# Half of a selective scan moved beside the relative-bias attention, and softmax division moved behind the value product

## The chip, the cores and the metric

One NeuronCore of a Trainium2 chip runs the whole program; the metric is the device time in microseconds (us) of one execution. Eight sequences go through it one after another. PE is TensorE, DVE VectorE, ACT ScalarE, POOL GpSimd, SP the engine whose queue issues all DMAs here. "BANKS" is PSUM (eight banks of 128x512 f32, PS[0] to PS[7]), WF and WB hold all constants in SBUF.

## The reference, cut to what matters

A residual stream x of shape (8, 512, 128) passes eight layers. The two that the change concerns:

```python
x = x + _L0_attn_ref(_layernorm(x), ...)        # bidirectional selective scan (Mamba)
    # per direction, 256 channels x 16 states, 512 time steps
    h = jnp.exp(dlt[:, :, None] * A) * h + (dlt * xt)[:, :, None] * bt[:, None, :]
    y = jnp.einsum('bdn,bn->bd', h, ct)
    ...
    y = (ys.transpose(1, 0, 2) + Dp * xc) * jax.nn.silu(z)
x = x + _L1_attn_ref(_layernorm(x), ...)        # 16 heads of 64, no 1/sqrt(d), relative-position bias
    attn = softmax(q @ k.T + bias[bucket(k - q)]);  out = (attn @ v) @ Wo
x = x + _L2_ffn_ref(_layernorm(x), ...)         # g1, be1, g2, be2 are layer norm gains and shifts
    x1 = _layernorm(x + attn_out, g1, be1)
    return _layernorm(x1 + moe_out, g2, be2)
```

## The kernel before

Each sequence goes through the stages moe0, attn1 (the relative-bias attention), lora1, heads (two attentions of 16 heads of 8) and last (L2's experts, L3's memory layer and experts). Six sequences run in a loop, the seventh and eighth behind it; their tiles have the prefixes y and z. While sequence b is in heads, the scan of sequence b+1 runs beside it (`mamba_scan`); its inputs were made beside the previous last stage (`mamba_pre`). The eighth has no successor: its stages run without a scan. So seven scans run beside heads, and the first runs alone (stage s0).

**The order of work.** Every engine has one queue in program order. Where two streams share a stage, each is a generator that yields nominal times, and `in_turn` merges them by these times when the program is built. The nominal times set the order and nothing else; on the chip every engine takes its queue in order and waits on semaphores.

**The scan** has 64 steps: 2 directions x 2 channel tiles x 16 states. Step m needs a decay exp(delta*A) (ACT, L754), a drive du*B (for even steps PE spreads the row of B over the partitions, L729, and DVE multiplies, L795; for odd steps a DMA brings the row and POOL multiplies, L766), the recurrence itself (DVE, L804), the product with the row of C (POOL, L770), and PE adds the product into the PSUM bank SUM by an identity matmul (L737, two passes). After 16 states DVE empties SUM (`flush`).

**attn1** handles 64 units of one head and 128 queries: PE makes a score tile (L2075), DVE adds the bias from a Toeplitz tile in `toep` and takes the row minimum (L2177), ACT exponentiates and sums the row into `den` (L2148), DVE takes the reciprocal (L2182) and multiplies the 128x512 tile `prob` by it (L2184), PE transposes it (L2082), ACT copies it to `probt` (L2156), and PE weighs the values with it (L2096, L2111). Eight units are a pair of heads; per pair PE also makes q, k and v (L2046, L2050), ACT moves them (L2127, L2130) and empties the weighed tile PS[5] to `ot` (L2137), and PE projects it (L2057) into PS[6], which adds up over all pairs; DVE adds it to X once (L2187). After step 64 of 72 only the last units' transposes, weighing and projection are left.

**last** begins with the norm ln1 (gain g1, shift be1), whose result goes through PE and ACT/DVE copies to XT, and has a norm ln2 (gain g2, shift be2) after the first experts, then XO = X + XN, a copy X <- XM (the next sequence), and ln3.

Of the kernel before, what the change touches and what calls it, by code (L numbers as in the profile page):

```python
# [18 lines left out]
ALU = mybir.AluOpType  # L19
# [19 lines left out]
H = 16  # L39
# [32 lines left out]
def bass_mk_seq(nc, x, cols_f, cols_b, ends, wf, wb, lora, lora_cols, onehot, table, w2, out):  # L72
# [35 lines left out]
    bc_dram = nc.dram_tensor("bc_rows", [2, 2 * NS, SEQ], F32, kind="Internal").ap()  # L108
    bias_dram = nc.dram_tensor("bias_line", [H, 1024], F32, kind="Internal").ap()
# [284 lines left out]
    def norm_parts(st, tag, src, dst, small, at, dst_t=None, banks=None, rms=False, sq=None, gain_t=None, gain=None,  # L394
                   shift=None, after=None, spare=None, idle=0, later=(), scaled_by_act=False):
# [12 lines left out]
        def vector(dve):  # L408
# [19 lines left out]
            if scaled_by_act:  # L428
                for j in range(NJ):
                    last = V.tensor_scalar(dst[:, j, :], src[:, j, :], s_mv[:, j, 0:1], None, ALU.subtract)  # L430
                last.then_inc(centred, 1)
            else:
                yield at + 3.2
                dve.wait_ge(rooted, 1)
            for j in range(0 if scaled_by_act else NJ):
                if rms:
# [4 lines left out]
                if gain is None:  # L441
                    ins.then_inc(normed, 1)
            if gain is not None:
                link(ins)
                link(V.tensor_tensor(dst[:, :, :], dst[:, :, :], bc(gain.unsqueeze(1), [P, NJ, D]), ALU.mult))
                V.tensor_tensor(dst[:, :, :], dst[:, :, :], bc(shift.unsqueeze(1), [P, NJ, D]), ALU.add).then_inc(normed, NJ)  # L446
            if dst_t is not None:
                yield at + 4.6
                dve.wait_ge(turned, NJ)
                if gain_t is not None:  # L450
# [19 lines left out]
        def scalar(act):  # L470
# [10 lines left out]
            if gain_t is not None:  # L481
# [9 lines left out]
    def mamba_pre(st, fetch, delay=0.0, stretch=1.0):  # L491
# [19 lines left out]
        def sync(sp):  # L511
            yield -3.0
# [164 lines left out]
    def mamba_scan(st, dest, START, STEP):  # L677

        STEPS = 2 * ND * NS
# [16 lines left out]
        def step(i):  # L696

            return i // (ND * NS), i // NS % ND, i % NS
# [22 lines left out]
        def tensor(pe):  # L721
            for s in range(STEPS + LATE):
# [8 lines left out]
                if m >= 0:  # L731
                    n = m % NS
                    yield at(s) + 0.45 * STEP
                    pe.wait_ge(rd, m + 1)
                    if n == 0 and m:
                        pe.wait_ge(emptied, m // NS)
                    nc.tensor.matmul(SUM, ident, work[:, m % RW, :], start=(n == 0), stop=(n == NS - 1)).then_inc(acc, 1)  # L737
# [8 lines left out]
        def scalar(act):  # L746
            for m in range(STEPS):
# [5 lines left out]
                a = (d * ND + t) * NS + n  # L753
# [18 lines left out]
        def vector(dve):  # L772
# [3 lines left out]
            def flush(q):  # L776
                d, t = q // ND, q % ND
                dve.wait_ge(acc, NS * (q + 1))
# [4 lines left out]
                dve.wait_ge(emptied, q)  # L783
                V.scalar_tensor_tensor(xc[:, 1, t, :], xc[:, 1, t, :], W("D")[:, ND + t:ND + t + 1], SUM,
                                       ALU.mult, ALU.add).then_inc(emptied, 1)
                dve.wait_ge(emptied, q + 1)
# [3 lines left out]
            for s in range(STEPS):  # L790
# [5 lines left out]
                if s >= NS and n == LATE:  # L796
                    yield at(s) + 0.2 * STEP
                    flush(s // NS - 1)
# [11 lines left out]
            V.tensor_tensor(dest[:, :, :], XIN[:, :, :], OUT.rearrange(tiles, j=NJ), ALU.add)  # L810

# [362 lines left out]
    def last_layers(st, copy_next):  # L1174
# [5 lines left out]
                         spare=PS[7], idle=10)  # L1180
# [8 lines left out]
        ln2 = norm_parts(st, "ln2", Y, XN, SMALL, 73.0, gain=W("g2"), shift=W("be2_2"))  # L1189
# [25 lines left out]
        def vector(dve):  # L1215
# [4 lines left out]
            nc.vector.tensor_tensor(XO[:, :, :], X[:, :, :], XN[:, :, :], ALU.add).then_inc(freed, 1)  # L1220
            if copy_next:
                dve.wait_ge(freed, 1)
                nc.vector.tensor_copy(X[:, :, :], XM[:, :, :])
            for layer in (ln3, memo, ln4, moe3):
# [348 lines left out]
    def back_parts(st, tag, heads, O, turned_o, w_o, add_to, banks, at, bias=None):  # L1573
# [21 lines left out]
        def gpsimd(pool):  # L1595
            if bias is not None:
                yield at - 24.0
                nc.gpsimd.tensor_tensor(add_to[:, :, :], add_to[:, :, :], bc(bias.unsqueeze(1), [P, NJ, D]), ALU.add).then_inc(biased, 1)

# [244 lines left out]

    with Stage("p0") as st:
# [16 lines left out]
    def layers(b, scan_next, pre_next):  # L1862
# [113 lines left out]
        with Stage("attn1") as st:  # L1976
# [5 lines left out]

            PAIR = 2 * NJ
            U, NPAIR = H * NJ, H // 2
            EXP, TURN = 2, 4
            MAKE_AT = {0: 0, 2: 1, 4: 2}
            WEIGH_AT = {5: 0, 7: 1, 1: 2, 3: 3}
            EMPTY_AT, PROJECT_AT = 4, 6  # L1990
            LAST = U + PAIR
            NS_, NP_, NT_ = 4, 6, 2 * PAIR
            RING = (PS[4], PS[7])
            qk = st.sb("qk", [P, 2, 2, SEQ])
# [417 lines left out]
```

## Time and profile before

| | us |
|---|---|
| median of 3 runs | 5484.77 |
| lowest, highest | 5479.66, 5489.24 |
| the profiled execution, its span | 5479.63, 5477.8 |

The profiled execution took 1.8 us more than the span of its instructions. A view of windows has a line for each stretch: its length, then the busy us (and number of instructions) of PE, PE's weight loads, DVE, ACT and POOL, the mean granted TensorE clock as a share of 2.4 GHz, the DMA engines' busy share, and GB/s. A view of groups has line, engine, operation, tiles and shapes, count, then total busy us and mean ns of one, then the engine's idle us ahead of them and who ended it. A timeline has start and duration in us. Engines are pipelined, so a next instruction of the same engine may start up to about 0.1 us before the one ahead ends by the record.

### The profile page before, as it was taken

To read this page: it belongs to the slowest core of one execution; us is meant where nothing else is said; L and a number is where in the kernel's file an instruction comes from. 1 tells how busy PE (TensorE), PEld (TensorE's weight loads), DVE (VectorE), ACT (ScalarE), POOL (GpSimd) and SP (SyncE) were. 2 spreads that over 40 slices of the span, in tenths; PEclk is the share of its full clock that TensorE was granted. 3 is DMA by queue.
4 is the path that set the end of the run, shared out by engine and by line. 5 is a ranking of instruction groups with operands and counts; after the bars stand their busy time and mean duration, and the time that the engine had idled before them with its cause. 6 is when DMAs were issued, how large, how long until landed. Compare 5 with 4: busy or idle time off the path is not lost. (4 is left out here: it accounts for less than half of the span.)

```text
span 5477.8 us, 69802 instructions
## 1 busy us (share of the span) xinstructions
PE 4692.1 (86%) x22038; PEld 2198.6 (40%) x22038; DVE 3509.5 (64%) x8259; ACT 2756.3 (50%) x5134; POOL 1480.0 (27%) x1876
## 2 busy tenths in 40 slices
PE   4679897998889887898878988799887998989888
PEld 2134344443444324443344433454334443444344
DVE  5766856668556784667755687556865568466445
ACT  2256553555536554375542655446654465436453
POOL 2712720136100461106401074011730127200200
PEclk8899998999989999899989999899988999999799
DMA  3411320123101231013210132001320113201000
GB/s 131 148 35 59 117 63 1 47 67 114 48 3 55 75 110 34 3 55 98 87 34 16 41 120 83 17 30 47 123 68 9 36 58 114 66 2 55 1 28 7
DMA packets 150490, 315.67 MB, mean 58 GB/s; under 512 B 16209, under 2 KB 24913, under 8 KB 150113
## 3 DMA queue, kind: packets, MB, share of 16 engines
q1 hardware_dynamic: 150128, 311.17, 17.9%
q8 instruction: 189, 3.10, 0.2%
q14 instruction: 173, 1.41, 0.1%
HBM read 307.89 MB, written 3.21 MB: 57 GB/s over the span
## 5 line engine op out<-in xcount | busy, mean ns | idle before, releaser
L196 PE MATMUL BANKS<-WB 128*128 128x512 bf16 x1616 | 448.0, 428 | 188.2 <-DVE XN L446 56.5
L770 POOL TENSOR_TENSOR heads_work<-heads_work,heads_c_all 128x512 f32<-128x512 f32 x384 | 487.1, 1271 | 325.3 <-DVE heads_work L804 312.6
L1516 ACT ACTIVATE heads_prob<-BANKS 128x512 f32<-128x512 f32 (+3 forms) x768 | 376.8, 518 | 284.6 <-PE BANKS L1411 278.2
L212 POOL TENSOR_TENSOR rstd<-rstd,WF 128x4 f32<-128x4 f32 x24 | 24.2, 1007 | 1658.2 <-DVE rstd L230 1658.2
L737 PE MATMUL BANKS<-heads_work,WF 128*128 128x512 f32 x768 | 441.0, 660 | 0.4
L196 PEld LDWEIGHTS BANKS<-WB 128*128 128x128 bf16 x1616 | 165.3, 107 | 432.1 <-issue 199.5
L406 POOL TENSOR_TENSOR rstd<-rstd,WF 128x4 f32<-128x4 f32 x48 | 48.5, 1010 | 938.5 <-DVE rstd L427 937.7
L1411 PE MATMUL BANKS<-heads_parts_kT,heads_parts_qT 64*128 64x512 bf16 (+3 forms) x768 | 237.8, 359 | 67.9 <-DVE heads_nmax L1557 47.3
L1554 DVE CUSTOM_DVE_ANT_0 BANKS<-BANKS,WF 128x384 f32<-128x384 f32 (+3 forms) x512 | 243.4, 502 | 68.9 <-PE BANKS L1411 65.6
L2156 ACT COPY attn_probt<-BANKS 128x512 f32<-128x512 f32 x384 | 223.9, 583 | 126.1 <-PE BANKS L2082 123.7
L2177 DVE CUSTOM_DVE_ANT_0 attn_biased<-BANKS,attn_toep 128x512 f32<-128x512 f32 x384 | 263.1, 685 | 34.1 <-DMA attn_toep<-bias_line 25.4
L2148 ACT ACTIVATE attn_prob<-attn_biased,attn_nmax 128x512 f32<-128x512 f32 x384 | 280.2, 730 | 1.1 <-DVE attn_nmax L2177 1.0
L882 PEld LDWEIGHTS BANKS<-last_x_w,last_x_a 128*128 128x128 f32 x1536 | 211.5, 203 | 171.7 <-ACT last_x_a L922 89.8
L882 PE MATMUL BANKS<-last_x_w,last_x_a 128*128 128x128 f32 x1536 | 219.8, 289 | 66.5 <-ACT last_x_a L922 66.5
L1557 DVE TENSOR_REDUCE heads_nmax<-BANKS 128x1 f32<-128x512 f32 x384 | 248.2, 680 | 36.9 <-PE BANKS L1411 35.2
L804 DVE TENSOR_TENSOR_SCAN heads_work<-BANKS,heads_work 128x512 f32<-128x512 f32 x192 | 233.4, 1215 | 32.6 <-POOL heads_work L766 32.6
L766 POOL TENSOR_TENSOR heads_work<-heads_b_all,m_du 128x512 f32<-128x512 f32 x192 | 244.6, 1274 | 13.7 <-DMA heads_b_all<-bc_rows 13.5
L2082 PEld LDWEIGHTS BANKS<-WF,attn_prob 128*128 128x128 f32 x1536 | 163.3, 140 | 209.2 <-DVE attn_prob L2184 134.7
L2082 PE MATMUL BANKS<-WF,attn_prob 128*128 128x128 f32 x1536 | 240.1, 281 | 6.7 <-ACT attn_probt L2156 3.7
L795 DVE TENSOR_TENSOR BANKS<-BANKS,m_du 128x512 f32<-128x512 f32 x256 | 179.6, 702 | 101.4 <-PE BANKS L729 99.7
L754 ACT ACTIVATE BANKS<-m_delta,WF 128x512 f32<-128x512 f32 x256 | 177.1, 692 | 106.6 <-DVE s_work L804 87.6
L1411 PE MATMUL BANKS<-heads_qm,heads_parts_kT 64*128 64x512 bf16 (+3 forms) x768 | 215.3, 357 | 13.4 <-DVE heads_nmax L1554 10.0
(892 smaller groups left out, 10541.3 us busy)
## 6 DMA issues: line engine op xcount, KB each, us to landing
heads_c_all<-bc_rows SPq DMA_DIRECT2D x384, 256.0 KB, 3.2
heads_b_all<-bc_rows SPq DMA_DIRECT2D x192, 256.0 KB, 3.6
attn_toep<-bias_line SPq DMA_DIRECT2D x96, 448.0 KB, 4.3
last_x_w<-in_w SPq DMA_DIRECT2D x48, 512.0 KB, 3.8
s_c_all<-bc_rows SPq DMA_DIRECT2D x64, 256.0 KB, 3.3
yheads_c_all<-bc_rows SPq DMA_DIRECT2D x64, 256.0 KB, 3.1
s_b_all<-bc_rows SPq DMA_DIRECT2D x32, 256.0 KB, 3.7
yheads_b_all<-bc_rows SPq DMA_DIRECT2D x32, 256.0 KB, 3.5
```

Source lines behind the costliest of these rows:

```text
L196: nc.tensor.matmul(bank, ident_b, bc(ident_b[:, 0:1], [P, SEQ]), start=True, stop=True)
L737: nc.tensor.matmul(SUM, ident, work[:, m % RW, :], start=(n == 0), stop=(n == NS - 1)).then_inc(acc, 1)
L766: nc.gpsimd.tensor_tensor(work[:, s % RW, :], b_all[:, k % RB, :], du[:, d, t, :], ALU.mult).then_inc(drv[1], 1)
L770: nc.gpsimd.tensor_tensor(work[:, m % RW, :], work[:, m % RW, :], c_all[:, m % RC, :], ALU.mult).then_inc(rd, 1)
L882: last = nc.tensor.matmul(DOWN[e % 2][:, j * D:(j + 1) * D], a1[:, i % 3, j * P:(j + 1) * P], down_part(i), start=(t == 0 and j == 0), sto ...
L1411: nc.tensor.matmul(take(kind, i)[:, lo:hi], left[rows, P * tile:P * (tile + 1)], right[rows, lo:hi], start=True, stop=True).then_inc(sem, 1)
L1516: nc.scalar.activation(prob[:, i % PR, lo:hi], bank("T", i)[:, lo:hi], ACT.Exp).then_inc(exped, 1)
L1554: V.tensor_tensor_reduce(got, got, W("early")[:, SEQ - hi:], -1.0, BIG, ALU.add, ALU.min, nmax[:, j, h:h + 1]).then_inc(maxed, 1)
L1557: V.tensor_reduce(nmax[:, j, h:h + 1], got, AX.X, ALU.max, negate=True).then_inc(maxed, 1)
L2082: last = nc.tensor.transpose(bank[:, kt * P:(kt + 1) * P], prob[:, u % NP_, kt * P:(kt + 1) * P], ident)
L2148: nc.scalar.activation(prob[:, e % NP_, :], biased[:, e % NS_, :], ACT.Exp, bias=nmax[:, e:e + 1], scale=-1.0, accum_out=den[:, e:e + 1]). ...
L2177: V.tensor_tensor_reduce(biased[:, s % NS_, :], PS[s % NS_], toep[:, h % 4, c:c + SEQ], -1.0, BIG, ALU.add, ALU.min, nmax[:, s:s + 1]).the ...
```

## The change

Steps 0 to 31 of the scan (direction 0) now run in stage attn1 as `mamba_early`, steps 32 to 63 stay in heads, where their nominal step grows from 3.4 to 6.78. `mamba_early` leaves PE out: all rows of B and C come by DMA (into XNM, XTM, XO, XN, free at that time), POOL makes all drives and C products and also adds them up, in XM. It has two work tiles and one bank for the decay. In the attention, transposition takes `prob` undivided; DVE takes eight reciprocals at once, two DMAs write them as rows to DRAM (`norm_rows`), one DMA reads them back spread over 64 partitions each (`weights`), and DVE divides when it empties PS[5]. DVE takes over one of three copies to `probt`; each pair's projection goes through the ring of PS[4] and PS[7] and is added to X by DVE. In last, ln1's gain and shift are applied to the transposed copy and, afterwards, to the tile; ln2's gain is one operand of its scaling and its shift be2 is added to X by POOL in heads; the copy X <- XM stands behind ln3; XIN's load stands ahead of the expert weights in SP's queue.

```diff
+                if gained is not None:
+                    ins = V.scalar_tensor_tensor(dst[:, j, :], dst[:, j, :], s_rstd[:, j:j + 1], gained, ALU.mult, ALU.mult)
...
+                if columns is not None:
+                    V.tensor_scalar(dst_t[:, HALF:], banks[1][:, HALF:], columns[0], columns[1], ALU.mult, ALU.add).then_inc(ready, 1)
...
+    def mamba_early(st, K, START, STEP):
+        work = st.sb("e_work", [P, 2, SEQ])
+        b_rows = XNM[:, :, :].rearrange(line), XTM[:, :]
+        c_rows = XO[:, :, :].rearrange(line), XN[:, :, :].rearrange(line)
+        total = XM[:, :, :].rearrange(line)
+        DECAY = PS[6]
...
+            def fetch_b(m):
+                if m >= 2:
+                    sp.wait_ge(driven, m - 1)
+                sp.dma_start(b_rows[m % 2], row(0, m)).then_inc(b_ld[m % 2], 16)
...
+            def fetch_c(m):
+                if m >= 2:
+                    sp.wait_ge(multiplied, m - 1)
+                sp.dma_start(c_rows[m % 2], row(1, m)).then_inc(c_ld[m % 2], 16)
...
+            for m in range(K + 1):
+                if m < K:
+                    yield at(m) - 2.6 * STEP
+                    fetch_b(m)
+                if m >= 1:
+                    yield at(m - 1) - 1.5 * STEP
+                    fetch_c(m - 1)
...
+        def scalar(act):
+            for m in range(K):
+                yield at(m) - 0.6 * STEP
+                if m:
+                    act.wait_ge(scanned, m)
+                a = m
+                nc.scalar.activation(DECAY, delta[:, 0, m // NS, :], ACT.Exp, scale=W("A")[:, a:a + 1]).then_inc(decayed, 1)
...
+            def drive(m):
+                pool.wait_ge(b_ld[m % 2], 16 * (m // 2 + 1))
+                if m >= 2:
+                    pool.wait_ge(added, sums(m - 1))
+                    pool.wait_ge(multiplied, m - 1)
+                nc.gpsimd.tensor_tensor(work[:, m % 2, :], b_rows[m % 2], du[:, 0, m // NS, :], ALU.mult).then_inc(driven, 1)
...
+                    pool.wait_ge(scanned, m + 1)
+                    pool.wait_ge(c_ld[m % 2], 16 * (m // 2 + 1))
+                    nc.gpsimd.tensor_tensor(work[:, m % 2, :] if n else total, work[:, m % 2, :], c_rows[m % 2],
+                                            ALU.mult).then_inc(multiplied, 1)
...
+                    if n:
...
+                        pool.wait_ge(multiplied, m + 1)
+                        pool.wait_ge(added, sums(m))
+                        nc.gpsimd.tensor_tensor(total, total, work[:, m % 2, :], ALU.add).then_inc(added, 1)
+                if m + 2 < K:
...
+                    drive(m + 2)
...
+                dve.wait_ge(driven, m + 1)
+                dve.wait_ge(decayed, m + 1)
+                V.tensor_tensor_scan(work[:, m % 2, :], DECAY, work[:, m % 2, :], 0.0, ALU.mult, ALU.add).then_inc(scanned, 1)
+    def attn1_parts(st, copy_by_act):
+        def at(s):
+            return 2.05 * s
...
+        def denominators(sp):
+            for w in range(NPAIR):
+                yield at(PAIR * w + 10) + 0.5
+                sp.wait_ge(inverted, w + 1)
...
+                    for a in range(2):
+                        sp.dma_start(bass.AP(home.tensor, home.offset + a * SEQ, [[1, P], [P, NJ]]),
+                                     rden[:, PAIR * w + a:PAIR * (w + 1):2]).then_inc(put, 16)
+                yield at(PAIR * w + 13) + 1.0
+                sp.wait_ge(put, 32 * (w + 1))
+                if w:
+                    sp.wait_ge(emptied, w)
+                sp.dma_start(weights[:, :], bass.AP(home.tensor, home.offset, [[SEQ, 2], [0, DK], [1, SEQ]])).then_inc(spread, 16)
...
+            def empty(w):
+                dve.wait_ge(weighed, w + 1)
+                dve.wait_ge(spread, 16 * (w + 1))
...
+                V.tensor_tensor(ot[:, w % 2, :].rearrange(split, j=NJ)[:, :, ::-1], PS[5].rearrange(split, j=NJ),
+                                weights[:, :].rearrange(split, j=NJ), ALU.mult).then_inc(emptied, 1)
...
+    EARLY = 32
...
+            streams = [mamba_early(st, EARLY, 8.2, 4.18)] if scan_next else []
+            streams.append(attn1_parts(st, (1, 1, 0)))
...
-            streams = [mamba_scan(st, XM, 4.0, 3.4)] if scan_next else []
+            streams = [mamba_scan(st, XM, 4.0, 6.78, EARLY)] if scan_next else []
```

**DVE in attn1, first pair of heads.** Before, each unit's bias tile (L2177, two rows each) is followed by the reciprocal and the scaling of the unit ahead of it:

```order
L2182 RECIPROCAL attn_rden<-attn_den 128x1
L2184 TENSOR_SCALAR attn_prob<-attn_prob,attn_rden 128x512
L2177 ISA attn_biased,attn_nmax<-BANKS,attn_toep 128x512
L2177 ISA attn_nmax 128x1
L2182 RECIPROCAL attn_rden<-attn_den 128x1
L2184 TENSOR_SCALAR attn_prob<-attn_prob,attn_rden 128x512
```

Now (L1199 is the bias tile, L921 the recurrence, L1213 a copy of a transposed tile):

```order
L921 SCALAR_TENSOR_TENSOR attn_e_work<-BANKS,attn_e_work 128x512
L1199 ISA attn_biased,attn_nmax<-BANKS,attn_toep 128x512
L1199 ISA attn_nmax 128x1
L1199 ISA attn_biased,attn_nmax<-BANKS,attn_toep 128x512
L1199 ISA attn_nmax 128x1
L921 SCALAR_TENSOR_TENSOR attn_e_work<-BANKS,attn_e_work 128x512
L1199 ISA attn_biased,attn_nmax<-BANKS,attn_toep 128x512
L1199 ISA attn_nmax 128x1
L1213 COPY attn_probt<-BANKS 128x512
```

Reciprocal and scaling are gone from between the bias tiles, a recurrence stands after every second one and a copy after every third.

**POOL in attn1.** It had nothing here before. Now drive (L894), product with C (L904) and sum (L910) alternate without a gap in the queue:

```order
L904 TENSOR_TENSOR attn_e_work<-attn_e_work,XO 128x512
L910 TENSOR_TENSOR XM<-XM,attn_e_work 128x512
L894 TENSOR_TENSOR attn_e_work<-XNM,m_du 128x512
L904 TENSOR_TENSOR attn_e_work<-attn_e_work,XN 128x512
L910 TENSOR_TENSOR XM<-XM,attn_e_work 128x512
```

Three POOL instructions stand there for each of the 32 steps.

**SP in attn1, one pair of heads.** Before, the queue had only the 16 loads of `toep` (L2034). Now:

```order
L1027 DMA norm_rows<-attn_rden 128x4x1 x2
L861 DMA XNM<-bc_rows 128x512
L866 DMA XN<-bc_rows 128x512
L861 DMA XTM<-bc_rows 128x512
L866 DMA XO<-bc_rows 128x512
L1033 DMA attn_weights<-norm_rows 128x1x512
L861 DMA XNM<-bc_rows 128x512
L866 DMA XN<-bc_rows 128x512
L1016 DMA attn_toep<-bias_line 128x896 x2
```

Rows of B (L861) and C (L866) stand behind the write of the reciprocals, and behind the wait for it that comes ahead of L1033.

## Rows read from the trace of the kernel before

**Rows 1.** Windows: attn1 of sequence 2; heads with a scan; heads of the eighth.

```profile
1017.50:1150.60 133.10, 129.74 (x672) 62.20 (x670) 78.94 (x257) 98.78 (x225) 0.00 (x0) 1.00 0.17 56
1166.80:1410.60 243.80, 215.17 (x1042) 76.33 (x1042) 193.52 (x376) 145.02 (x274) 152.15 (x209) 0.95 0.34 104
5106.70:5294.10 187.40, 161.05 (x870) 58.37 (x870) 99.17 (x271) 105.42 (x210) 34.40 (x113) 0.76 0.00 1
```

**Rows 2.** Groups of instructions in attn1, 1018 to 1150.5.

```profile
L2148 ACT ACTIVATE attn_prob<-attn_biased,attn_nmax 128x512 f32<-128x512 f32 x64 | 46.7, 730 | 0.2 <-DVE attn_nmax L2177 0.2
L2177 DVE CUSTOM_DVE_ANT_0 attn_biased<-BANKS,attn_toep 128x512 f32<-128x512 f32 x64 | 43.8, 685 | 5.4 <-PE BANKS L2075 4.4 <-DMA attn_toep<-bias_line 0.3
L2156 ACT COPY attn_probt<-BANKS 128x512 f32<-128x512 f32 x64 | 37.3, 583 | 21.0 <-PE BANKS L2082 20.6
L2184 DVE TENSOR_SCALAR attn_prob<-attn_prob,attn_rden 128x512 f32<-128x512 f32 x64 | 31.2, 487 | 2.3
L2182 DVE RECIPROCAL attn_rden<-attn_den 128x1 f32<-128x1 f32 x64 | 10.4, 162 | 38.3 <-ACT attn_prob L2148 37.9
```

**Rows 3.** Timeline of PE in attn1: score tiles eight units apart.

```profile
1084.02 1.13 PE L2075 MATMUL BANKS<-attn_qk 64*128 64x512 f32 x4
...
1100.15 1.13 PE L2075 MATMUL BANKS<-attn_qk 64*128 64x512 f32 x4
```

**Rows 4.** Timeline of attn1: first product; last bias tile, last sum.

```profile
1016.93 1.96 PE L2046 MATMUL BANKS<-XT,WF 128*128 128x512 f32 x4 [0.30 <-PEq L206]
...
1138.24 0.68 DVE L2177 CUSTOM_DVE_ANT_0 attn_biased<-BANKS,attn_toep 128x512 f32<-128x512 f32 x1
...
1150.53 0.69 DVE L2187 TENSOR_TENSOR X<-X,BANKS 128x512 f32<-128x512 f32 x1 [9.28 <-PE BANKS L2057]
```

**Rows 5.** POOL: two in the scan alone; C products there; a dependent chain.

```profile
117.98 1.27 POOL L766 TENSOR_TENSOR s_work<-s_b_all,m_du 128x512 f32<-128x512 f32 x1
119.21 2.66 POOL L770 TENSOR_TENSOR s_work<-s_work,s_c_all 128x512 f32<-128x512 f32 x2
...
L770 POOL TENSOR_TENSOR s_work<-s_work,s_c_all x64: 1260/1267/1282, 115.4 to 244.6; 128x512 f32<-128x512 f32 x64
...
1202.36 0.26 POOL L1529 CAST heads_parts<-heads_nmax 128x16 bf16<-128x16 f32 x1 [0.66 <-DVE heads_nmax L1554]
1202.69 0.23 POOL L1532 TENSOR_TENSOR heads_nmax<-heads_nmax,heads_parts 128x16 f32<-128x16 f32 x1
```

**Rows 6.** Groups of the scan in heads, 1166.8 to 1410.6.

```profile
L737 PE MATMUL BANKS<-heads_work,WF 128*128 128x512 f32 x128 | 73.1, 656 | 0.1
L804 DVE TENSOR_TENSOR_SCAN heads_work<-BANKS,heads_work 128x512 f32<-128x512 f32 x32 | 38.9, 1216 | 5.5 <-POOL heads_work L766 5.5
L795 DVE TENSOR_TENSOR BANKS<-BANKS,m_du 128x512 f32<-128x512 f32 x32 | 22.6, 705 | 12.4 <-PE BANKS L729 12.2
```

**Rows 7.** Windows within the first attention of heads: eighth sequence; second.

```profile
5142.00:5178.00 36.00, 32.52 (x167) 9.59 (x171) 20.90 (x79) 18.65 (x44) 13.45 (x49) 0.50 0.00 1
1215.00:1251.00 36.00, 33.09 (x177) 10.31 (x177) 29.88 (x83) 21.13 (x47) 28.52 (x56) 0.92 0.32 101
```

**Rows 8.** DMA queue, and issues: KB each, median us to landing.

```profile
q1 hardware_dynamic: 150128, 311.17, 17.9%
...
heads_b_all<-bc_rows SPq DMA_DIRECT2D x192, 256.0 KB, 3.6
XIN<-in_x SPq DMA_DIRECT2D x8, 256.0 KB, 5.8
bc_rows<-p_rows_bc SPq DMA_DIRECT2D x4, 64.0 KB, 1.6
```

**Rows 9.** Timeline of DVE at ln2 of the second sequence.

```profile
1519.56 0.69 DVE L445 TENSOR_TENSOR XN<-XN,WF 128x512 f32<-128x512 f32 x1
1520.36 0.69 DVE L446 TENSOR_TENSOR XN<-XN,WF 128x512 f32<-128x512 f32 x1
...
1521.81 0.43 DVE L1223 COPY X<-XM 128x512 f32<-128x512 f32 x1
```

More of the change, by code:

```diff
@@ L394, in norm_parts @@
     def norm_parts(st, tag, src, dst, small, at, dst_t=None, banks=None, rms=False, sq=None, gain_t=None, gain=None,
-                   shift=None, after=None, spare=None, idle=0, later=(), scaled_by_act=False):
+                   shift=None, after=None, spare=None, idle=0, later=(), scaled_by_act=False,
+                   columns=None, gained=None):
         s_stats, s_mv, s_rstd = small
@@ L440, in vector @@
                                           ALU.subtract, ALU.mult)
[L441 to L446, printed above, removed]
+                ins.then_inc(normed, 1)
             if dst_t is not None:
@@ L480, in scalar @@
             act.wait_ge(turned, NJ // 2)
-            if gain_t is not None:
+            if columns is not None:
+                nc.scalar.activation(dst_t[:, 0:HALF], banks[0][:, 0:HALF], ACT.Identity, scale=columns[0],
+                                     bias=columns[1]).then_inc(ready, 1)
+            elif gain_t is not None:
                 nc.scalar.activation(dst_t[:, 0:HALF], banks[0][:, 0:HALF], ACT.Copy, scale=gain_t).then_inc(ready, 1)
@@ L694, in decay, with step @@
             return PS[2] if m % 2 else (XNM[:, :, :].rearrange("p j d -> p (j d)"), XTM[:, :])[m // 2 % 2]
-        def step(i):
+        def step(m):
+            i = first + m
             return i // (ND * NS), i // NS % ND, i % NS
@@ L731, in tensor @@
                 if m >= 0:
-                    n = m % NS
+                    n = step(m)[2]
                     yield at(s) + 0.45 * STEP
+                    if m == 0 and n:
+                        nc.tensor.matmul(SUM, ident, XM[:, :, :].rearrange("p j d -> p (j d)"), start=True, stop=False)
                     pe.wait_ge(rd, m + 1)
                     if n == 0 and m:
-                        pe.wait_ge(emptied, m // NS)
+                        pe.wait_ge(emptied, (first + m) // NS - BEGUN)
                     nc.tensor.matmul(SUM, ident, work[:, m % RW, :], start=(n == 0), stop=(n == NS - 1)).then_inc(acc, 1)
@@ L777, in flush @@
                 d, t = q // ND, q % ND
-                dve.wait_ge(acc, NS * (q + 1))
+                dve.wait_ge(acc, NS * (q + 1) - first)
                 if d == 0:
@@ L795, in vector @@
                     V.tensor_tensor(DRIVE, DRIVE, du[:, d, t, :], ALU.mult).then_inc(drv[0], 1)
-                if s >= NS and n == LATE:
+                if first + s >= NS * (BEGUN + 1) and n == LATE:
                     yield at(s) + 0.2 * STEP
-                    flush(s // NS - 1)
+                    flush((first + s) // NS - 1)
                 yield at(s) + 0.5 * STEP
@@ L2005, in layers @@
-            weighed, emptied, projected = (st.sem(n) for n in ("weighed", "emptied", "projected"))
-            def unit(u):
-                return u // PAIR, u % PAIR // 2, u % 2
-            def made_in(s):
-                i = MAKE_AT.get(s % PAIR)
-                if i is None or s >= U:
-                    return None
-                r = s // PAIR + (i < 2)
-                return (r, i) if r < NPAIR else None
-            place = {("make", 0, 0): 0, ("make", 0, 1): 1}
-            for s in range(LAST):
-                if 0 <= s - TURN < U:
-                    place["turn", s - TURN] = len(place)
-                if made_in(s):
-                    place[("make",) + made_in(s)] = len(place)
```

494 lines of the change are left out of this document (310 added, 184 removed).

## The prediction

> **What bounds the kernel now.** I read the views from coarse to fine: the stages first, then what fills each of the two that trade work.
>
> The windows [rows 1] give the stages. attn1 takes 133.1 us, PE is busy for 129.7 of them at the full clock, DVE for 79, POOL not at all: PE bounds it, and DVE and POOL have room. Heads with a scan beside it takes 243.8 us, without one (eighth sequence) 187.4. So 64 scan steps cost heads 56.4 us, 0.88 us a step, where nothing is saturated in the mean (PE 88%, DVE 79%, POOL 62%): the cost is queueing behind each other. The change moves half of the steps from a stage where they cost this much to one where PE has no time to give but they don't use PE.
>
> In the timeline of PE, eight units of attn1 take 16.13 us back to back [rows 3], 2.02 us a unit. The same work stays on PE.
>
> **The change, part by part.**
>
> *Heads loses 32 steps.* PE loses 64 passes of 0.656 us, 42 us; DVE 32 recurrences of 1.216 and 16 products of 0.705, 50 us [rows 6]. On the line between the two windows, half of the steps are worth half of 56.4, 28.2 us. That line bends with the clock: the eighth sequence had a mean clock of 0.76 where the second had 0.95, and 36 us of its first attention ran at 0.50, the lower level, 1.2 GHz, with PE's scan work gone from the gaps [rows 1, 7]. If the 161 us of PE there had run at 0.95, up to 161 x (1 - 0.76/0.95) = 32 us would have been saved, heads without a scan would be 155, and half of the difference is 44 us. If, the other way, half a scan already lets the clock fall as far, up to 16 us of the 28 are lost, and 12 stay. Ends 12 and 44; I take 30, near the line, since PE keeps half of the filling work. Seven sequences: -210 us.
>
> *attn1 gets 32 steps.* PE has none of their work. DVE loses 64 scalings (31.2 us) and 64 reciprocals (10.4), gets 32 recurrences (38.9), 21 copies and 16 tiles of divisions and sums (some 0.69 each, like the bias tile that reads PSUM; 25 us) [rows 2]: 79 - 42 + 64 = 101 of 133. ACT loses a third of its 64 copies (12.3) and eight emptyings (4.7) and gets 32 decays of about 0.73: 98.8 + 6 = 105. Neither becomes the bound. POOL does 3 x 32 tiles of 1.27 us, 122 us, and sets a pace. Independent POOL tiles start 1.23 us apart; in a chain on POOL the next one starts 0.07 us after the end instead of 0.04 ahead of it [rows 5], so the two dependent ones of a step cost 0.11 more each: 3 x 1.23 + 0.22 = 3.91 us a step. In stage s0, 64 products stand between 115.4 and 244.6, 4.10 us for each three POOL tiles that lie there, 1.11 times their 3.69 [rows 5]; with that loss 4.34. PE's pace is 16.13/8 x 4.18/2.05 = 4.11 us for the units that the order puts beside one step. The queues tie both together, so a step takes the longer: ends 4.11 and 4.34, I take 4.25.
>
> The first recurrence needs its row of B. Ahead of it in SP's queue stand four loads of 448 KB. The queue took 17.9% of 16 engines for 311 MB [rows 8], 50.4 us of one engine per MB; 2.1 MB over 16 engines are 6.6 us, the rest of a landing 2.8 (3.6 less 0.8 for its own 256 KB), a drive 1.3: recurrence 0 comes 10.7 us after PE's first product. The last bias tile stands behind recurrence 29, 10.7 + 29 x 4.25 = 134.0 us in, where it now comes at 1138.24 - 1016.93 = 121.3 [rows 4]: +12.7.
>
> *The tail.* From the start of the last bias tile to the end of the last sum it is 13.0 us now [rows 4], PE's own work for the most part. After the change a second chain runs beside it: bias tile 0.77, exponential 0.93 with its sum, reciprocal 0.16, the two writes, the read, the division 0.69, projection some 1.1, sum 0.69. The trace has no write of 1024 single numbers. Lower end: a write of 64 KB lands in 1.6 us; upper end: 64 packets per engine at the queue's mean of 0.104 us (15.7 ms of one engine over 150,128 packets), 6.7, and 2.8 to land, 9.5 [rows 8]. I take 4, since 4 bytes are far from a mean packet. The read is 256 KB: 3.6 us like a row, or 5.8 like XIN; I take 5.8, as it queues behind rows. Sum 14.2: +1.2, ends 0 and 6.7. The scan's own end, 10.7 + 31 x 4.25 and some 5 us of products, sum and flush, is at 147, that of the attention at 148: just hidden.
>
> So attn1 grows by 13.9 in seven sequences and 1.2 in the eighth: +98 us. Before the last pairs the write and read have ten steps of cover, so they cost nothing there; SP's wait for the write comes 7.1 us of nominal time after its issue, above the 4 taken. A row has from its issue two steps less its own POOL tile, 8.5 - 1.3 = 7.2 us, against 3.6 to land. If that cover goes, POOL waits, then the recurrence behind it in DVE's queue, then the bias tiles behind that, then PE.
>
> *last.* ln1 and ln2 each lose a multiplication and an addition of 0.69 us on DVE, with nothing beside them [rows 9]; in ln1 they come back behind the copy to XT, where DVE waits for the gate products. ln2's subtractions lie beside POOL's inverse root. The copy X <- XM, 0.35 net, leaves the path. 3.2 us in eight sequences: -25; ends 0 (another chain ends last) and -30. The earlier XIN load and one more POOL tile in heads: nothing, POOL idles there for 92 us.
>
> **The sum.** 5479.6 - 210 + 98 - 25 = 5343. The median of the runs is 5.1 us above the profiled execution: 5348.
>
> **Rivals.**
>
> *The read back runs on few DMA engines.* 256 KB are 13.2 us of one engine; over 16 that is 0.8 us, over two 6.6, 5.8 us later. The tail then grows by another 3.6 (9.4 against 5.8), 29 us in eight sequences. Rows issued right behind it have part of their packets behind it: 5.8 late against a spare of 3.6, POOL waits 2.2 us in six pairs of seven sequences, 92 us: 5469. For it: it is the one load whose source pattern has an outermost count of 2, so nothing in the trace is like it. Against: rows stand at varying distance behind it, and one that comes 3 us later meets half of it. The Trainium skill, "DMA: Bandwidth & Descriptors", section "Why a DMA increments its semaphore by 16 and not by 1", says that the number of engines is the largest, up to 16, that divides the outermost counts of both patterns; here that would be 2. By that rule the sum would be this rival's 5469; no load of this trace shows it.
>
> *Heads gives back less* (15 instead of 30 us, the clock falls as in the eighth sequence): 5348 + 105 = 5453. For it: the windows at 0.50 and 0.92 [rows 7]. Against: half of PE's filling work stays.
>
> *More than that*: heads gives 40 and attn1 keeps PE's 4.11: 5348 - 70 - 7 x 29 x 0.14 = 5250.
>
> *Slower: the one decay bank.* Decay m+1 waits for recurrence m, and recurrence m+1 for decay m+1. If each time an exponential and a copy stand ahead on ACT (0.93 + 0.58) and two bias tiles on DVE (1.54), a step is 0.73 + 1.22 + 1.51 + 1.54 + 0.2 = 5.2 us: 29 x 0.95 x 7 = +193, 5541. It decides from a pace of 4.25 + 137/203 = 4.92 us. Against: the queues run ahead while POOL, which needs 3.9 of every 4.25 us, keeps the others waiting.
>
> *No change*: the gain is eaten by parts of these at once, about 5485.
>
> **How the numbers follow.** Forecast 50% (own range 5290 to 5400), read on few engines 14%, heads gives less 10%, more 13%, slower 8%, no change 5%. The likeliest gives 5348. The range 5250 to 5470 holds the first four nearly whole and leaves out some 2 in 10. A change of 0.2% (11 us) is about what a measurement can tell. The first four are faster, 0.87; no change is 0.05, slower 0.08.
>
> **What the profile after would show.** attn1 of about 147 us with POOL at some 83% and the recurrences 4.25 us apart; a pace above 4.6 with DVE waiting for ACT's decay speaks for the bank. Idle time of POOL ended by rows of B or C, and a read that lands after 9 us instead of 4 to 6, speak for few engines. Heads of about 214 us with a clock above 0.85; a clock near 0.75 and 228 us mean that the return was lost there. In last, the gate of ln1 starts 1.4 us earlier. The prediction is wrong above all if the pace of attn1 or the clock in heads is: 0.1 us of pace is 20 us in the end.

## The result and the profile after

| us | before | changed |
|---|---|---|
| median of 4 runs | 5482.22 | 5576.18 |
| lowest, highest | 5471.41, 5489.24 | 5567.91, 5592.56 |
| span of the profiled execution | 5477.8 | 5590.5 |

The ratio is 1.017, interval 1.015 to 1.020: slower by 94 us, where 5348 was forecast and the range ended at 5470.

The windows after, over the stretches of [rows 1]: attn1 of sequence 2, heads with a scan, heads of the eighth.

```profile
1035.80:1223.50 187.70, 142.25 (x672) 66.06 (x670) 103.03 (x207) 104.29 (x228) 118.67 (x94) 0.89 0.53 141
1239.70:1446.20 206.50, 179.19 (x959) 65.12 (x962) 146.47 (x325) 123.97 (x242) 93.93 (x162) 0.93 0.20 62
5220.60:5408.20 187.60, 161.20 (x863) 58.18 (x866) 99.01 (x271) 105.44 (x210) 35.44 (x114) 0.75 0.00 1
```

Heads fell from 243.8 to 206.5 us, more than the 30 forecast, and kept a clock of 0.93. attn1 grew from 133.1 to 187.7. DVE is busy for 103 us of it, ACT for 104, POOL for 119, as forecast (101, 105, 122): the work was counted rightly. No engine is full, so the 40 us above the forecast are waiting.

Waits in that attn1: engine, tile and line, what it waited for, us in total, times, the longest.

```profile
DVE attn_e_work L921 <- POOL attn_e_work L894: 37.1, 18, 9.1
...
POOL attn_e_work L894 <- DMA XNM<-bc_rows: 23.7, 8, 11.3
...
PE BANKS L1078 <- DVE attn_ot L1185: 21.2, 5, 15.1
...
POOL attn_e_work L894 <- DMA XTM<-bc_rows: 17.2, 5, 6.7
...
POOL attn_e_work L904 <- DMA XN<-bc_rows: 8.2, 4, 3.1
POOL attn_e_work L904 <- DMA XO<-bc_rows: 6.7, 5, 2.4
```

POOL waits 56 us for rows (one wait, 11.3, is the start), DVE's recurrence for POOL, and PE for the division that frees its bank. The recurrences of this stage start 5.24 us apart in the mean, where 4.25 was forecast. So rows of B and C come late. The DMA issues of the page: KB each, median us from issue to landing.

```profile
attn_toep<-bias_line SPq DMA_DIRECT2D x96, 448.0 KB, 6.5
XNM<-bc_rows SPq DMA_DIRECT2D x112, 256.0 KB, 7.7
XTM<-bc_rows SPq DMA_DIRECT2D x112, 256.0 KB, 6.9
XO<-bc_rows SPq DMA_DIRECT2D x112, 256.0 KB, 8.1
XN<-bc_rows SPq DMA_DIRECT2D x112, 256.0 KB, 8.3
heads_b_all<-bc_rows SPq DMA_DIRECT2D x96, 256.0 KB, 3.5
```

The same 256 KB from the same tensor land in 3.5 us in heads ([rows 8] has 3.6) and in 7 to 8 in attn1. The forecast had 3.6 and a spare of 3.6: the spare is used up in the median. What shares the queue only in attn1, beside the bias lines, are the writes of the reciprocals (L1027) and the read of them (L1033). The end of the eighth sequence's attn1, where no row is in the queue, shows both alone. A read here is the time from its issue (SPq L1033) to the division on DVE that waits for it (L1185). The timeline of SP's issues and DVE:

```profile
5179.85 0.51 SPq L1033 DMA_DIRECT2D zattn_weights<-norm_rows  x1
...
5182.94 0.91 SPq L1027 DMA_DIRECT2D norm_rows<-zattn_rden  x2
...
5194.27 0.69 DVE L1185 TENSOR_TENSOR zattn_ot<-BANKS,zattn_weights 128x512 f32<-128x512 f32 x1 [9.98 <-DMA zattn_weights<-norm_rows]
...
5195.03 0.51 SPq L1033 DMA_DIRECT2D zattn_weights<-norm_rows  x1
...
5202.25 0.69 DVE L1185 TENSOR_TENSOR zattn_ot<-BANKS,zattn_weights 128x512 f32<-128x512 f32 x1 [2.58 <-DMA zattn_weights<-norm_rows]
```

The last read takes from 5195.03 to 5202.25, 7.2 us, with nothing beside it; the one before it, with a pair of writes issued 3 us behind it, takes 14.4. The DMA's own two rows for 5194.5 to 5202.5, in 40 slices: the busy share of 16 engines in tenths, and GB/s.

```profile
DMA  0000000041111112011111111111111111100000
GB/s 0 0 0 0 0 0 0 0 82 31 41 61 41 61 41 51 20 41 51 51 51 51 51 51 51 51 51 51 51 51 51 51 51 51 51 31 20 0 0 0
```

The whole queue is at 51 GB/s and a busy share of 0.1: two engines of 16 would be 0.125.

### The profile page after: what moved, and what is told of

The parts are those of the page before. It is cut to its first block and busy times, and to the rows that moved or that the text cites. A ratio compares the mean times of both kernels' runs of the same rounds, so it can differ in the third digit from the quotient of the medians.

```text
span 5590.5 us, 68903 instructions
## 1 busy us (share of the span) xinstructions
PE 4513.1 (81%) x21380; PEld 2145.2 (38%) x21478; DVE 3335.9 (60%) x7491; ACT 2633.8 (47%) x4902; POOL 1904.6 (34%) x2206
## 5 line engine op out<-in xcount | busy, mean ns | idle before, releaser
L1931 ACT ACTIVATE heads_prob<-BANKS 128x512 f32<-128x512 f32 (+3 forms) x768 | 364.4, 520 | 203.8 <-PE BANKS L1826 199.4
L921 DVE TENSOR_TENSOR_SCAN attn_e_work<-BANKS,attn_e_work 128x512 f32<-128x512 f32 x192 | 234.4, 1221 | 215.7 <-POOL attn_e_work L894 211.5
L1108 PE MATMUL BANKS<-WF,attn_prob 128*128 128x128 f32 x1536 | 255.5, 292 | 131.7 <-DVE attn_probt L1213 123.6
L1199 DVE CUSTOM_DVE_ANT_0 attn_biased<-BANKS,attn_toep 128x512 f32<-128x512 f32 x384 | 256.7, 680 | 155.6 <-PE BANKS L1100 113.1
L783 POOL TENSOR_TENSOR heads_work<-heads_work,heads_c_all 128x512 f32<-128x512 f32 x192 | 243.2, 1268 | 294.4 <-DVE heads_work L818 293.8
L1078 PE MATMUL BANKS<-attn_probt,attn_vals 128*64 128x512 f32 x768 | 230.3, 686 | 113.8 <-DVE attn_ot L1185 111.4
L1161 ACT COPY attn_probt<-BANKS 128x512 f32<-128x512 f32 x258 | 149.6, 580 | 192.5 <-PE BANKS L1108 192.2
L1100 PE MATMUL BANKS<-attn_qk 64*128 64x512 f32 x768 | 234.6, 690 | 4.1 <-ACT attn_qk L1139 4.1
L750 PE MATMUL BANKS<-heads_work,WF 128*128 128x512 f32 x384 | 233.5, 692 | 0.0
L910 POOL TENSOR_TENSOR XM<-XM,attn_e_work 128x512 f32<-128x512 f32 x180 | 228.5, 1270 | 14.1
L1336 ACT ACTIVATE last_x_a<-BANKS,WF 128x512 f32<-128x512 f32 x192 | 128.7, 686 | 182.7 <-PE BANKS L1308 181.5
```

The costliest lines, as they stand in the source:

```text
L783: nc.gpsimd.tensor_tensor(work[:, m % RW, :], work[:, m % RW, :], c_all[:, m % RC, :], ALU.mult).then_inc(rd, 1)
L921: V.tensor_tensor_scan(work[:, m % 2, :], DECAY, work[:, m % 2, :], 0.0, ALU.mult, ALU.add).then_inc(scanned, 1)
L1100: nc.tensor.matmul(PS[(s + a) % NS_], q[:, j * P:(j + 1) * P], k, start=True, stop=True).then_inc(scored, 1)
L1108: last = nc.tensor.transpose(bank[:, kt * P:(kt + 1) * P], prob[:, u % NP_, kt * P:(kt + 1) * P], ident)
L1199: V.tensor_tensor_reduce(biased[:, s % NS_, :], PS[s % NS_], toep[:, h % 4, c:c + SEQ], -1.0, BIG, ALU.add, ALU.min, nmax[:, s:s + 1]).the ...
L1931: nc.scalar.activation(prob[:, i % PR, lo:hi], bank("T", i)[:, lo:hi], ACT.Exp).then_inc(exped, 1)
```

## The experiments

Stage lengths below are from the first instruction of attn1's norm to that of the next norm, in sequences 1 to 6: 140 us before, 191 to 197 in the changed kernel; the eighth, without a scan, 140 and 156. Four theories: the *read* on two engines holds up the rows (R); *SP* stands still while it waits for the write and the emptied bank and issues rows late (S); scan and attention *couple* through the decay bank (C); and, from the second group on, the *writes* themselves (W). A stage's tail is the time from the start of its last bias tile to the next norm: 13.3 us before. Where a run leaves out the read, the weighed tile is multiplied by a constant tile, so the probabilities aren't divided, and nothing in the tail waits for the writes.

**The read on 16 engines.**

```diff
-                sp.dma_start(weights[:, :], bass.AP(home.tensor, home.offset, [[SEQ, 2], [0, DK], [1, SEQ]])).then_inc(spread, 16)
+                for a in range(2):
+                    sp.dma_start(weights[DK * a:DK * (a + 1), :],
+                                 bass.AP(home.tensor, home.offset + a * SEQ, [[0, DK], [1, SEQ]])).then_inc(spread, 16)
```

> The read back of the reciprocals is made by two transfers, one per head, whose source pattern has an outermost count of 64 instead of 2; nothing else changes. Theory R (the read runs on two DMA engines and holds up the rows of the scan behind it): the read lands some 4 us sooner, POOL's waits for rows go from some 56 us of one attn1 to below 20, attn1 with a scan falls from 195 to 160-170 us, without one from 156.5 to 150-153, the whole to about 5330-5390 us. Theory S (SP's own queue: it stands still while it waits for the write and for the emptied bank, and the rows are issued late): attn1 stays at 185-195, the whole at 5510-5570. Theory C (scan and attention hold each other up on DVE and ACT, through the single decay bank): no change, 5560-5590.

Measured: 5454.1 us, ratio 0.994 (0.992 to 0.996): 122 us faster than the changed kernel by this edit alone, and still 64 us above the upper end that R gave. attn1 is 173 to 181 (R gave 160 to 170), the eighth 146 (150 to 153), and POOL still waits 35 us for rows, the start included, where R gave below 20. The same two rows for 5070 to 5078, the last read there:

```profile
DMA  0000000000000449896500000000000000000000
GB/s 0 0 0 0 0 0 0 0 0 0 0 0 0 61 82 205 215 358 195 174 21 0 0 0 0 0 0 0 0 0 0 0 0 0 0 0 0 0 0 0
```

The 256 KB move in 1.6 us at up to 358 GB/s instead of in 5.7 at 51. SP's waits for the writes and the emptied bank are 36 us of one attn1 in the changed kernel and 37 here, so the gain isn't theirs. R holds, but is not all.

**No read; no DMA for the reciprocals at all.** In the first the line L1033 and DVE's wait for it go, in the second `denominators` as a whole; the weighed tile is multiplied by the constant `W("Wo")` in both.

> Leaves out the read of the reciprocals; the weighed tile is multiplied by a constant tile instead, so the probabilities are not divided. The writes and both waits of SP (for the write, for the emptied bank) stay. Theory R: at or a little below the time with the read on 16 engines, 5300-5370 us, attn1 155-165. Theory S: 5480-5570, since SP stands still as before. Theory C: 5540-5590.

> Leaves out the writes, the read and SP's waits for them; the weighed tile is multiplied by a constant tile. The scan beside the attention stays. What is left of attn1's growth is the scan's own. Theories R and S: attn1 with a scan 150-158 us, without one 142-146, the whole 5250-5320 us. Theory C: attn1 with a scan still above 180, the whole above 5450.

Measured: 5434.3 (0.991, 0.989 to 0.993), between what R and S gave, and 5327.0 (0.972, 0.970 to 0.975). The read on 16 engines costs 20 us, part of them the tail's wait for writes and read (the eighth is 140 without it, 146 with it), everything around the writes 107, and what is left is the scan beside the attention: attn1 of 160 to 163 us, a few above what R and S gave and far below C's 180. The rows of B and C land in 3.1 to 3.3 us there, beside the same bias lines: these aren't what makes them late. The windows without any of these DMAs, attn1 and heads:

```profile
999.60:1155.80 156.20, 136.30 (x672) 64.33 (x670) 102.69 (x207) 103.57 (x228) 119.12 (x94) 0.97 0.49 155
1172.00:1376.40 204.40, 176.72 (x970) 64.71 (x969) 146.44 (x326) 124.27 (x242) 93.87 (x162) 0.95 0.20 62
```

**All of the scan in heads again.** `EARLY = 0`, `mamba_scan(st, XM, 4.0, 3.4, EARLY)`, no `mamba_early`.

> All 64 steps of the scan beside heads again, at the step of before (3.4), nothing beside the attention; the reciprocals still go by the two writes and the read. Shows what the new attention costs without rows in the queue. If the eighth sequence speaks for all (attn1 156.5 against 139.7): 5482 + 8 x 17 - 25 = 5593 us by every theory that puts the eighth's loss down to the tail and the writes; if the long attn1 comes from the new attention alone and not from the rows, attn1 would be 195 in all and the whole near 5870; if the eighth is an exception and the others lose nothing without rows, 5460-5480.

Measured: 5552.8 (1.013, 1.011 to 1.015), attn1 150 to 158; none of the three expected times came true, the first was 40 us too long. The new way to divide costs 10 to 18 us a sequence with no row in the queue. Most of it is the tail, 24 us in every sequence instead of 13.3, 86 us in the eight. The last pair of heads of the eighth sequence; the timeline of SP's issues and DVE:

```profile
5145.85 1.84 SPq L1027 DMA_DIRECT2D norm_rows<-zattn_rden  x2
...
5155.95 0.50 SPq L1033 DMA_DIRECT2D zattn_weights<-norm_rows  x1
...
5163.70 0.69 DVE L1185 TENSOR_TENSOR zattn_ot<-BANKS,zattn_weights 128x512 f32<-128x512 f32 x1 [3.81 <-DMA zattn_weights<-norm_rows]
```

The read is issued 10.1 us behind the writes, for which SP waits, and the division comes 7.8 us later; the forecast had 4 and 5.8. So the DMAs for the reciprocals cost twice: in the tail, where they are waited for, and where they meet the rows. In the changed kernel 5576 - 5327 = 249 us are theirs; its eight attn1 stages are 252 us longer than without them, 70 in the tails and the rest ahead of the tails, most of it in the seven sequences with rows in the queue.

**Only the writes, and SP never waits for them before it must.** No read; SP waits for a pair's writes before the next pair's, and not for the emptied bank.

> Leaves out the read, and SP waits for a pair's writes only before the writes of the next pair; it does not wait for the emptied bank. The weighed tile is multiplied by a constant tile. With no DMA for the denominators the kernel takes 5327 us, with the writes and both waits of SP 5434. If the writes themselves (1024 elements of 4 bytes for each pair) hold up the rows: 5410-5440, rows that land 4-5 us after their issue. If SP's standing still was the cost (rows issued late): 5325-5350, rows that land in some 3.3 us as without the writes.

Measured: 5460.1 (0.995, 0.993 to 0.997), not faster than with SP's waits (5434) but 26 us slower, and above the range given for the writes too. S falls as the reason for the 107 us: it is the writes. Why the waits helped isn't settled; perhaps they keep a row or two out of the stretch behind the writes. That stretch, 1078 to 1090, begins with a pair of writes issued at 1078.46:

```profile
DMA  9999788998421499524074043932949040422000
GB/s 430 410 399 382 290 314 294 206 148 93 36 2 41 164 191 123 164 96 82 0 27 14 0 27 20 27 14 7 27 7 14 0 14 0 14 7 14 7 7 7
```

From 1083.7 on 0 to 27 GB/s pass, while rows of 256 KB are waiting. Of the 37 packets of 2 KB that start there 30 take 0.4 to 2.5 us in the trace, instead of the 0.084 that is the median elsewhere.

**The same writes, 64 bytes apart.**

```diff
-                        sp.dma_start(bass.AP(home.tensor, home.offset + a * SEQ, [[1, P], [P, NJ]]),
+                        sp.dma_start(bass.AP(home.tensor, home.offset + 16 * a * SEQ, [[16, P], [16 * P, NJ]]),
```

> As the one with only the writes (5460 us; no read, weighed tile multiplied by a constant tile), but the elements of 4 bytes lie 64 bytes apart in DRAM instead of side by side. If it is the many small pieces that share a line of memory that hold up the rows behind them: 5330-5370, rows that land in some 3.5 us. If it is their number or size, whatever their place: 5440-5475, and row packets that take 500 to 2000 ns behind each pair of writes as before.

Measured: 5333.1 (0.973, 0.970 to 0.976), within the uncertainty of no writes at all. The same number of pieces of 4 bytes, but none beside another. Rows and writes land in

```profile
XNM<-bc_rows SPq DMA_DIRECT2D x112, 256.0 KB, 3.4
...
norm_rows<-attn_rden SPq DMA_DIRECT2D x96, 2.0 KB, 3.2
```

3.4 and 3.2 us. The last two writes of the eighth, with nothing beside them, land in 2.0 us; side by side, without the early scan, in 8.9. So W is right in a narrow form: what costs is that 512 neighbouring words are written as separate pieces. Whether it is words right beside each other, or all of them within 2 KB, a single distance can't tell, and what the memory does then no run shows. Nor was a kernel run that divides rightly with the writes apart and the read on 16 engines.

**Reciprocals by TensorE, no DMA; with fewer early steps; with the first rows earlier.** PE multiplies a column of reciprocals, taken 64 times, with the identity, and ACT copies the result to `weights`:

```diff
+            def rows(w):
+                bank = ring(("rows", w))
+                pe.wait_ge(inverted, w + 1)
+                for u in range(PAIR):
+                    j, a, v = u // 2, u % 2, PAIR * w + u
+                    last = nc.tensor.matmul(bank[DK * a:DK * (a + 1), j * P:(j + 1) * P], bc(rden[:, v:v + 1], [P, DK]),
+                                            ident, start=True, stop=True, skip_group_check=True)
```

> The reciprocals are brought to the rows by TensorE: for each pair 8 products of a column of reciprocals, taken 64 times, with the identity, into a bank of the ring, and a copy by ACT into the same tile of weights; no writes, no read. Computes the same as the changed kernel. Without any bringing it is 5327 us. PE gets 4 x 8 passes of 128 columns (some 0.16 us each, a quarter of the 0.656 us of a 512-column pass), 5.2 us a sequence and ACT 4 copies of 0.58: if all of it lies on the path 5327 + 8 x 5.2 = 5369 and with ACT's 5387; if PE's waits take half of it 5345. Above 5450 the turn in the ring itself would be the cost, and DMA not the cheapest part that could be mended.

> As the one with the reciprocals by TensorE, with 28 steps beside the attention instead of 32 and 36 (step 6.04) beside heads. If the scan's end sets the end of attn1 (last recurrence 9 us behind the last bias tile's start, at 4.2 us a step): attn1 falls by 8 to 15 us, heads rises by 4 x 0.6 to 4 x 1.2 us, the whole falls by 20 to 85 us against the one of 32. If the pace of the attention beside any scan sets it: attn1 falls by 2-4 us, heads rises by as much, no change or +15.

> As the one with the reciprocals by TensorE, with the first rows of B and C issued ahead of the bias lines of heads 2 and 3. If the start of the scan counts (first recurrence 15.2 us after attn1's start, its row waits behind 4 x 448 KB): it comes 3 us sooner and the whole falls by 7 x 2-3 = 14 to 21 us. If the pace alone sets the end, no change (within 8 us).

> Reciprocals by TensorE, first rows ahead of the bias lines of heads 2 and 3, 24 steps beside the attention and 40 (step 5.44) beside heads. With 32 steps and this order it was 5355 us, with 28 and the old order 5331. If each step in heads still costs about 1 us (28 against 32: heads 4 us longer) and attn1 gets 1.2 us shorter for each step that leaves it, as its bias tiles are then 4 x 1 us less slowed: 5290-5320. If attn1 no longer shrinks since its tail is already PE's own: 5325-5350.

> The same with 20 steps beside the attention and 44 (step 4.95) beside heads. If the cost of a step is the same in both stages by now: equal to 24 steps within 15 us. If heads' cost a step (0.6 to 1.2 us) is above attn1's: 10 to 30 us slower than 24 steps; if it is below: 10 to 30 us faster.

> Reciprocals by TensorE, first rows of B and C ahead of the bias lines of heads 2 and 3, 28 steps beside the attention and 36 beside heads. If the two gains add (5381 - 26 - 50): 5300-5315 us. If the early start was worth something only while the scan's end set attn1's end (32 steps), it is worth nothing here: 5325-5340.

| steps beside attn1 | first rows earlier | us | ratio (interval) | attn1 | heads |
|---|---|---|---|---|---|
| 32 | no | 5380.6 | 0.980 (0.979 to 0.982) | 166 | 220 |
| 32 | yes | 5354.7 | 0.976 (0.974 to 0.977) | 165 | 221 |
| 28 | no | 5330.5 | 0.971 (0.968 to 0.973) | 158 | 224 |
| 28 | yes | 5328.1 | 0.972 (0.971 to 0.974) | 158 | 224 |
| 24 | yes | 5418.8 | 0.988 (0.984 to 0.991) | 156 | 238 |
| 20 | yes | 5402.6 | 0.985 (0.982 to 0.988) | 154 | 235 |

(Stages: medians of the profiled execution in us; heads from the norm ahead of it to its last sum, 259 before.) The expectation of the first row counted 4 pairs of heads; there are 8, and the 54 us above 5327 are 8 x 6.7. With 28 steps the kernel beats both: 5328 against 5481 before. Two expectations failed. The early rows gave 26 us at 32 steps, a little over the 14 to 21 (and nothing at 28, so the gains don't add). And with 24 steps the whole was 5419, 91 us slower than with 28, where 5290 to 5350 was given: attn1 fell by 2 us, but heads rose by 14 for 4 steps, and by less for 8. Heads' order of instructions changes with its nominal step. With 24 steps, windows over two of the heads stages show 241.0 us at a granted clock of 0.90 and 233.0 at 0.95, so some of it goes with the clock; why 40 steps fit heads so badly is open.

**The decay bank.** Both with no DMA for the reciprocals and the constant tile. First the decays take turns between the bank and an SBUF tile, and decay m+1 waits for recurrence m-1; then all go to an SBUF tile, with the wait of the changed kernel.

```diff
-        DECAY = PS[6]
+        DECAY = PS[6], st.sb("e_decay", [P, SEQ])[:, :]
```

> As the one without any DMA for the denominators (5327 us; weighed tile multiplied by a constant tile), but the decays go by turns into the bank and a tile in SBUF, so that decay m+1 waits for recurrence m-1. If the single bank couples ACT's and DVE's queues: pace from 4.2 to 4.0 us a step, 31 x 0.2 x 7 = 43 us less or more, 5230-5285. If POOL's three tiles a step set the pace: 5315-5335, drives still 3.99 us apart.

> As the one without any DMA for the denominators (5327 us; weighed tile multiplied by a constant tile), the single decay in an SBUF tile instead of the bank, each decay waits for the recurrence before it as in the changed kernel. If the place is what costs (DVE's recurrence and POOL's product stretch each other when the decay comes from SBUF): with every decay there, not every second, at least as slow as with two, 5385-5450, recurrences of up to 2.2 us. If the two-decay order itself was what cost: 5320-5340.

Measured: 5386.1 (0.982, 0.979 to 0.985) and 5489.3 (1.001, 1.000 to 1.002), against 5327: the first slower than both of its expectations, the second slower than its 5450 at most. The first changes wait and place together, the second the place alone, 162 us for all decays; the 59 us of the first fit half of the decays in SBUF, with no gain from the wait to be seen. One attn1 with all decays in SBUF, and one with the bank; columns: instructions | busy us, mean ns | idle ahead.

```profile
L921 DVE TENSOR_TENSOR_SCAN attn_e_work<-attn_e_decay,attn_e_work 128x512 f32<-128x512 f32 x32 | 61.7, 1930 | 10.6 <-POOL attn_e_work L894 9.4 <-ACT attn_e_decay L886 0.8
...
L910 POOL TENSOR_TENSOR XM<-XM,attn_e_work 128x512 f32<-128x512 f32 x30 | 52.6, 1753 | 2.3
```

```profile
L921 DVE TENSOR_TENSOR_SCAN attn_e_work<-BANKS,attn_e_work 128x512 f32<-128x512 f32 x32 | 39.0, 1219 | 8.1 <-POOL attn_e_work L894 5.8 <-ACT BANKS L886 2.3
...
L910 POOL TENSOR_TENSOR XM<-XM,attn_e_work 128x512 f32<-128x512 f32 x30 | 38.1, 1271 | 2.4
```

The recurrence grows from 1.22 to 1.93 us and POOL's sum from 1.27 to 1.75. With the bank, DVE waits 2.3 us for decays in the whole of attn1: rival C is refuted as a price of the wait. That two banks would be a little better isn't excluded; none was free, and it wasn't tried.

## Why the prediction was wrong, point by point

**Right, or near.** *Heads gives back 30* (ends 12 and 44): 37 (259.0 to 221.8), within the ends but 7 more. *last*, 3.2 a sequence: 220.6 before, 217.5 after. *The pace of the scan*, 4.25 us a step: 4.20 from recurrence to recurrence without the reciprocals' DMAs, with drives 3.99 apart when nothing stalls. *The last bias tile 12.7 later*: the bias tiles take 132.4 there instead of 118.1, 14.3 more. *Neither DVE nor ACT the bound*: so it is. Taken together, 5327 without the DMAs stands beside 5348 forecast, but partly by luck: heads fell by 284 us there instead of 210, attn1 grew by 150 instead of 98, and the two errors nearly cancel.

**The step that failed** is the sentence "Before the last pairs the write and read have ten steps of cover, so they cost nothing there". The time of the two transfers was covered; what they do to the others in the queue was not. It fails twice, and a third term, the tail, was too small.

First, the read. It was the rival "The read back runs on few DMA engines", at 14%, priced at 92 us for late rows and 29 for the tails, together 121 us; putting it on 16 engines gave 122. In the profiled executions the tails lose 29 us by that edit and the stages ahead of them 102, so not only the sum fits. Mechanism and price of the rival were right, and only the chance was wrong. A queue at 51 GB/s with a share of 0.1, where 16 engines reach 358, is what two engines would look like. By the rule of the Trainium skill, "DMA: Bandwidth & Descriptors", section "Why a DMA increments its semaphore by 16 and not by 1", it had to be two; the trace agrees. The argument against it ("rows stand at varying distance") was weaker than the rule.

Second, the writes. They were costed by their own landing alone: "Lower end: a write of 64 KB lands in 1.6 us; upper end: ... 9.5", taken as 4. They cost about 107 us with SP's waits around them, and the row in the trace nearest to them, contiguous pieces of 64 KB, could not show it: the price is in the rows behind them, whose packets took up to 2.5 us each. No rival had this. The Trainium skill, "DMA: Bandwidth & Descriptors", section "Specifications", says that below 512 B the engine reads, modifies and writes; the pieces 64 bytes apart are as small, and cost 6 us, within the uncertainty. Size alone is therefore not the price here.

Third, the tail: "Sum 14.2: +1.2, ends 0 and 6.7". In the eighth sequence, which has no scan beside it, the tail is 12.0 us longer in the changed kernel than before (25.3 against 13.3), 10.6 with all of the scan in heads, and 0.7 without the DMAs. Two of its terms were too small: 4 for the writes, where SP waited 10.1 us, and 5.8 for the read, which took 7.2 and 7.8. Also SP's wait for the writes was put at 7.1 us behind their issue; the yields give 3 x 2.05 + 0.5 = 6.65, and the writes need more than either, so SP stood still for 16.6 us in the attn1 of sequence 2.

The rival "Slower: the one decay bank" had a pace of 5.2 us and 5541; the pace came out at 5.24 and the time at 5576. That nearness is chance: POOL waited for rows, and DVE waited 0.2 us for decays.

**The rest of attn1.** The sum had "the scan's own end ... just hidden". POOL's last sum is indeed done before the attention, but the last flush (L926) stands in DVE's queue ahead of the division of the pair before the last. DVE's timeline, then PE's, without the reciprocals' DMAs:

```profile
1143.03 1.26 POOL L910 TENSOR_TENSOR XM<-XM,attn_e_work 128x512 f32<-128x512 f32 x1
...
1144.33 0.75 DVE L926 SCALAR_TENSOR_TENSOR m_du<-m_xc,WF,XM 128x512 f32<-128x512 f32 x1 [3.77 <-POOL XM L910]
...
1145.00 0.68 DVE L1184 TENSOR_TENSOR attn_ot<-BANKS,WF 128x512 f32<-128x512 f32 x1
```

```profile
1145.93 1.98 PE L1078 MATMUL BANKS<-attn_probt,attn_vals 128*64 128x512 f32 x4 [5.79 <-DVE attn_ot L1184]
```

DVE waits 3.8 us for the sum, the division that is ready stands behind it, and PE stands still for 5.8. The tail is 21.2 us in the mean of the seven sequences instead of 13.3, 55 us in all. With 28 steps and the reciprocals by TensorE it is 16.2, in the sequences with a scan as in the eighth: the flush has left the tail. So "hidden" has to be asked of the queue, not of the end times alone.

The account, changed kernel less before: without the DMAs attn1 has grown in the eight sequences together from 1121.8 to 1271.4 us (+150), heads has fallen from 2019.8 to 1736.0 (-284), last takes 25 less: -159, where the runs say 5327 - 5482 = -155. The writes with SP's waits add 107, the read on 16 engines 20, on two 122: +94.

## What to carry to other kernels

A transfer is costed twice: when it lands, and what the rows behind it in the same queue pay. Look at the outermost count of a broadcast read, and don't write neighbouring 4-byte words as separate pieces; a matrix product against the identity can turn and spread a column for 6.7 us of a sequence where two writes and a read, as they were written here, cost 31. When two chains share an in-order queue, ask of each waiting instruction what is ready behind it: moving a few steps out of the tail (28 for 32) gave more than the start did.

## What the runs showed of the hardware that was not expected

- Pairs of DMAs that write 512 words each, side by side, left the queue at 0 to 27 GB/s for some 6 us; the same words 64 bytes apart cost 6 us in the whole kernel, within the uncertainty, and landed in 3.2 us.
- One DMA with an outermost count of 2 moved at 51 GB/s, split in two with a count of 64 at up to 358.
- A recurrence whose decay lies in SBUF rather than in PSUM took 1.93 us instead of 1.22 beside a busy POOL, and POOL's sum 1.75 instead of 1.27. The Trainium skill, "SBUF — State Buffer", section "SBUF: two separate sides", has DVE with two SBUF inputs and GpSimd shut each other out; the runs agree: with the decay in PSUM neither is stretched (1.22 and 1.27).
- The granted clock of attn1 was 1.00 before [rows 1], 0.89 in the changed kernel, where PE waited most, and 0.97 without the DMAs; the same 672 matmuls were busy for 129.7, 142.3 and 136.3 us.
